# Rows loaded over 56 or 64 partitions instead of 53, and another order on VectorE, in a graph network's attention stage

## What is computed

```python
x = x * rsqrt(mean(x*x) + EPS) * rms_w          # 1250 x 1024
x = x @ W_down                                  # 1250 x 256
xl = (x @ Wl).reshape(n, 4, 64)                 # what a node sends
xr = (x @ Wr).reshape(n, 4, 64)                 # what a node adds as a receiver
# edges, and one loop for each node
msg = xl[src] + xr[dst]
act = where(msg > 0, msg, 0.2 * msg)
e = einsum('ehd,hd->eh', act, att)              # one score for each edge and head
m = segment_max(e, dst)
p = exp(e - m[dst])
out = segment_sum(p * xl[src], dst) / segment_sum(p, dst)
out = out.reshape(n, 256) @ W_up
```

## Time and profile before

| | |
|---|---|
| time before, median of 3 runs | 1694.56 us (1694.53 to 1698.33) |
| the profiled execution's own time | 1698.34 us |
| its span, first to last instruction | 1696.6 us |
| PE busy | 1495.4 us, 88% |
| DVE busy | 790.8 us, 47% |
| ACT busy | 442.5 us, 26% |
| POOL busy | 245.4 us, 14% |
| mean granted TensorE clock | 0.961 |

### The profile page before, as it was taken

The page is one execution under the profiler, slowest core; times in us unless marked ns, Lnnn a source line. Parts: engine busy times, 40 slices in busy tenths (PEclk is TensorE's granted clock), DMA queues, the critical chain, the costliest instruction groups (busy, mean ns, idle before and its releaser), DMA issues.

```text
span 1696.6 us, 19105 instructions
## 1 busy us (share of the span) xinstructions
PE 1495.4 (88%) x7184; PEld 1193.5 (70%) x7184; DVE 790.8 (47%) x1352; ACT 442.5 (26%) x723; POOL 245.4 (14%) x298
## 2 busy tenths in 40 slices
PE   3898999506888888887999999999999999999996
PEld 2887888505555555555888888888888888888885
DVE  6996665201666766675444375223113332321233
ACT  7762222103445454542111111002011000210000
POOL 1000000005455544530000001001000010000000
PEclk9997999857999999999999999999999999999998
DMA  1655343013444435432321365224006654410153
GB/s 42 176 166 183 121 104 103 18 49 110 129 156 135 123 106 166 135 96 85 123 107 50 104 229 213 86 96 149 1 0 211 199 174 149 155 37 1 59 183 105
DMA packets 100425, 196.57 MB, mean 116 GB/s; under 512 B 25550, under 2 KB 59638, under 8 KB 100334
## 3 DMA queue, kind: packets, MB, share of 16 engines
q1 hardware_dynamic: 75720, 121.00, 23.2%
q0 software_dynamic: 22992, 74.13, 12.7%
q10 hardware_dynamic: 1622, 0.22, 0.1%
HBM read 141.39 MB, written 53.92 MB: 115 GB/s over the span
## 4 chain that ended last, share of the span: by engine, by line
PE 52%; DVE 0%; ACT 0%; issue 0%; POOL 0%; DVEq 0%
PE layers_y_ps L1764 33%; PE layers_y_ps L1785 16%; PE layers_turn_ps L1748 2%; PE layers_up_ps L1732 2%; PE layers_y_ps L1801 1%; PE layers_turn_ps L1720 0%; PE layers_y_ps L1809 0%; DVE layers_parts_lo L1932 0%; DVE layers_y L1965 0%; POOL out L1705 0%; ACT layers_parts_hi L1876 0%; DVE layers_y L625 0%; DVE layers_y L2027 0%; DVE layers_ln_stats L2031 0%; DVE layers_ln_stats L619 0%
## 5 line engine op out<-in xcount | busy, mean ns | idle before, releaser
L1785 PE MATMUL layers_y_ps<-layers_parts_hi,layers_counts 128*128 128x512 f32 x464 | 143.6, 391 | 0.0
L1170 POOL DMA_INDIRECT attention_got<-xl_d,attention_src x128 | 126.5, 989 | 116.6 <-DVE attention_weighted L1415 69.7
L1785 PE MATMUL layers_y_ps<-layers_parts_lo,layers_counts 128*128 128x512 f32 x464 | 143.3, 390 | 0.0
L1764 PE MATMUL layers_y_ps<-layers_w_hi,layers_parts_hi 128*128 128x512 f32 x400 | 125.9, 396 | 0.0
L1764 PE MATMUL layers_y_ps<-layers_w_lo,layers_parts_hi 128*128 128x512 f32 x400 | 123.6, 390 | 0.0
L1764 PE MATMUL layers_y_ps<-layers_w_hi,layers_parts_lo 128*128 128x512 f32 x400 | 123.5, 390 | 0.0
L1170 POOL DMA_INDIRECT attention_got<-xl_d,heads_first_src x64 | 63.7, 995 | 411.9 <-issue 371.2
L1236 PE MATMUL attention_mix_ps<-attention_weighted,attention_hot 128*106 128x260 f32 x384 | 101.6, 399 | 5.2 <-DVE attention_weighted L1415 5.1
L1236 PEld LDWEIGHTS attention_mix_ps<-attention_weighted,attention_hot 128*106 128x106 f32 x384 | 66.4, 178 | 52.7 <-DVE attention_weighted L1415 24.3
L1201 PE MATMUL attention_row_ps<-attention_bent,edges_att_rows 128*128 128x512 f32 x192 | 102.5, 617 | 0.0
L1363 DVE TENSOR_TENSOR attention_bent<-attention_message_ps,attention_scaled 128x512 f32<-128x512 f32 x96 | 65.8, 686 | 74.0 <-ACT attention_scaled L1300 54.0
(11 more groups left out here) (306 smaller groups left out, 2904.3 us busy)
## 6 DMA issues: line engine op xcount, KB each, us to landing
layers_counts<-counts_d SPq DMA_DIRECT2D x30, 640.0 KB, 4.0
heads_dst_wide<-in_dst_held SPq DMA_DIRECT2D x25, 512.0 KB, 5.9
layers_rest<-x_d SPq DMA_DIRECT2D x23, 512.0 KB, 4.1
x_d<-layers_y POOLq DMA_DIRECT2D x20, 512.0 KB, 2.9
self_d<-layers_y POOLq DMA_DIRECT2D x20, 512.0 KB, 5.5
fetched_x<-x_d SPq DMA_DIRECT2D x17, 512.0 KB, 3.6
fetched_raw<-in_L_gnn_W_self POOLq DMA_DIRECT2D x16, 512.0 KB, 5.7
fetched_raw<-in_L_gnn_W_neigh POOLq DMA_DIRECT2D x16, 512.0 KB, 8.6
```

The source lines that it names most:

```text
L1170: pool.indirect_dma_start(got[s][:, t, :], None, xl_d, bass.IndirectOffsetOnAxis(src[s][:, t:t + 1], 0))\
L1764: last = nc.tensor.matmul(y_ps[n % 2][:, a:a + HALF], rows_in[t][:, k * P:(k + 1) * P], w[k][:, a:a + HALF], start=(k == 0 and p == 0), st ...
L1785: last = nc.tensor.matmul(y_ps[n % 2][:, a:a + HALF], counts[c % 2][:, k, :], part[k][:, a:a + HALF], start=(k == 0 and part is hi), stop= ...
```

## The change

Five edits. (1) `own_messages` reads and writes 56 partitions instead of 53 (`OWN_ROWS`). (2) `own_scores` takes 64 (`PART`) instead of 53, except for group 21, whose 39 rows stay; `last_scores` takes 25, 64 and 48 rows. (3) attention's xr rows are loaded over 64 partitions (32 for the last group). The rows beyond 53 belong to the next group; what they bring reaches no output. `summed` gets 64 partitions. (4) VectorE's order within a visit: both `weigh` go ahead of `bend` in unit 0, `take_max` 0 and 1 ahead of it in unit 2, `take_max` 3 and `take_best` ahead of it in unit 3, and `finish(j - 3)` moves from unit 1 to the end of unit 3. (5) ACT: `take_shifted` ahead of `keep_sums`.

```diff
+    LAST_ROW, OWN_ROWS = (BLOCKS - 1) * P, 56
...
         def own_messages(engine, first, end, heads):
-            span = slice(first * SUB, end * SUB)
-            own_xl = xl_d[span, :].rearrange("(j n) (h d) -> n j h d", n=SUB, h=HEADS)
             for h in heads:
-                engine.dma_start(summed[:, first:end, h, 0:HEAD_DIM], own_xl[:, :, h, :]).then_inc(g["own_loaded"], 16)
+                own_xl = bass.AP(xl_d.tensor, first * SUB * HID + h * HEAD_DIM,
+                                 [[HID, OWN_ROWS], [SUB * HID, end - first], [1, HEAD_DIM]])
+                engine.dma_start(summed[0:OWN_ROWS, first:end, h, 0:HEAD_DIM], own_xl).then_inc(g["own_loaded"], 16)
 
-        def own_scores(engine, first, end, nodes=SUB):
-            span = slice(first * SUB, first * SUB + (end - first) * nodes)
-            scores = loop_d[span, :].rearrange("(j n) (t k) -> t n j k", n=nodes, t=2)
+        def own_scores(engine, first, end, nodes=PART):
             for t in range(2):
-                engine.dma_start(best[t * PART:t * PART + nodes, first:end, :], scores[t])\
+                scores = bass.AP(loop_d.tensor, first * SUB * HEADS + t * KH,
+                                 [[HEADS, nodes], [SUB * HEADS, end - first], [1, KH]])
+                engine.dma_start(best[t * PART:t * PART + nodes, first:end, :], scores)\
                     .then_inc(g["own_loaded"], 16)
...
-                first, end = max(j * SUB, LAST_ROW), (j + 1) * SUB
+                first = max(j * SUB, LAST_ROW)
+                end = min(j * SUB + PART, first + 16 * ((ROWS - first) // 16))
...
+                held = min(PART, 32 * ((ROWS - j * SUB) // 32))
                 for part in range(2):
-                    sp.dma_start(xr[j % 3][part * PART:part * PART + SUB, :].bitcast(F32),
-                                 xr_d[part][j * SUB:(j + 1) * SUB, :]).then_inc(xr_ready[j % 3], 16)
+                    sp.dma_start(xr[j % 3][part * PART:part * PART + held, :].bitcast(F32),
+                                 xr_d[part][j * SUB:j * SUB + held, :]).then_inc(xr_ready[j % 3], 16)
...
                 if q == 3 and 1 <= j <= SUBS:
+                    take_shifted(j - 1)
                     keep_sums(j - 1)
-                    take_shifted(j - 1)
...
                 if q == 0 and 2 <= j <= SUBS + 1:
                     clamp(j - 2)
-                if i < LAST:
-                    bend(i)
-                if q == 0 and 2 <= j <= SUBS + 1:
                     weigh(j - 2, 0)
                     weigh(j - 2, 1)
-                if q == 1 and 3 <= j <= SUBS + 2:
-                    finish(j - 3)
                 if q == 2 and 1 <= j <= SUBS:
-                    for u in range(3):
-                        take_max(j - 1, u)
+                    take_max(j - 1, 0)
+                    take_max(j - 1, 1)
                 if q == 3 and 1 <= j <= SUBS:
                     take_max(j - 1, 3)
                     take_best(j - 1)
+                if i < LAST:
+                    bend(i)
+                if q == 2 and 1 <= j <= SUBS:
+                    take_max(j - 1, 2)
+                if q == 3 and 1 <= j <= SUBS:
                     find_edges(j - 1)
                     keep_best(j - 1)
+                if q == 3 and 3 <= j <= SUBS + 2:
+                    finish(j - 3)
```

More of the change, by code:

```diff
@@ L632, in front_stage @@
     EARLY, CLEAR, LAST_FILL = BLOCKS - 3, 4, 48
-    LAST_ROW = (BLOCKS - 1) * P
+    LAST_ROW, OWN_ROWS = (BLOCKS - 1) * P, 56
     with ExitStack() as ctx:
@@ L1422, in finish @@
                 b = j % 2
-                whole = summed[:, j]
+                whole = summed[0:SUB, j]
                 dve.wait_ge(keep_ready, j + 1)
@@ L2141, in graph_layers @@
                 best = m.sb("best", [P, SUBS, KH])
-                summed = m.sb("summed", [SUB, SUBS, HEADS, HEAD_DIM + 1])
+                summed = m.sb("summed", [PART, SUBS, HEADS, HEAD_DIM + 1])
                 first_src = m.sb("first_src", [P, SUB_TILES], I32)
```

## The result

The changed kernel takes 1618.49 us (median of 4, 1617.55 to 1622.2) against 1696.32 for the kernel before beside it: 0.9545 of it, 95% interval 0.9524 to 0.9566, and the medians are 77.8 us apart. 87.6 less (1607) was forecast; the range (1580 to 1634) held the time.

What follows compares the result with a forecast made beforehand. TensorE, 88% busy overall, was taken as the bound, with stalls where SP's issues held its queue. A 42.4, B 13.5, C 12.4 and D 19.3 sum to 87.6 us less, from 1694.56 to 1607; range 1580 to 1634.

Steps and rivals of the forecast that it cites:

- Spreading: Front's end: with 56 and 64 rows the six SP issues take 0.5 us each, over at 298 us instead of 351.
- A: Front's end, to take_heads(9): ACT takes the product at 318.3 us instead of 360.76, 42.4 us less.
- B: From take_heads(9) to attention's start: 10 us instead of 23.5, so 13.5 us less.
- C: Attention's start to the first clamp: gathers 6.4 us less, TensorE's clock 6 us less, 12.4 us less in all.
- D: Attention's visits, first to last clamp: the new order makes 350.1 us into 330.8, 19.3 us less.
- the one on POOL: Visits: POOL's indices come 4.3 us late, but it has room, its 8 gathers taking 10.3 us of the visit.
- the forecast's own ring: Visits: finish, store, dst_wide's landing, find_nodes, bend and finish again set the pace, 9.15 + w, 13.75 us instead of 14.76.
- w: Visits: the landing time of dst_wide behind the store, taken as 4.6 us.
- TensorE's 12.3 us a visit: Visits: without its two waits for VectorE, 2.45 us a visit, TensorE could do a visit in 12.3 us instead of 14.76.
- R2: Visits: the order brings nothing, w being 5.6 us or more; time 1617 to 1638 us, chance 0.3.
- R3: Front's end: the transfers do not spread or pieces hold the issue; about 1692 us, no change, chance 0.03.
- R4: Visits: slower than before through SP's late load, needing 18.4 us in each of 19 visits; chance 0.02.

Runs made afterwards that it cites:

- e1: The changed kernel with both orders (VectorE's and ACT's) as before, keeping edits 1 to 3: 1628.48 us, 0.9578 of the kernel before.
- e3: The changed kernel with SP's store of a group put behind the next group's load instead of ahead of it: 1573.54 us, 0.9276 of the kernel before.
- e9: The changed kernel itself once more, on the chip of the last group of runs: 1620.36 us, 0.9559 of the kernel before.
- e2: The changed kernel with 53 rows everywhere, keeping only the two new orders (edits 4 and 5): 1685.5 us, 0.9944 of the kernel before.
- e5: The changed kernel with the next group's source indices (src) alone issued ahead of the store: 1610.82 us, 0.9463 of the kernel before.
- e6: The changed kernel with the next group's dst_wide alone issued ahead of the store: 1628.1 us, 0.9572 of the kernel before.
- e8: The changed kernel with attention's xr rows loaded over 53 partitions as before: 1629.43 us, 0.9593 of the kernel before.
- e12: e3 with the store issued in two pieces of 48 and 5 rows, as in e7: 1562.54 us, 0.9217 of the kernel before.
- e10: The changed kernel with ACT's keep_sums ahead of take_shifted again: 1624.15 us, 0.9577 of the kernel before.
- e7: The changed kernel with the store issued in two pieces of 48 and 5 rows: 1612.01 us, 0.9487 of the kernel before.

## Why the prediction was right, and where not

**Spreading: right.** The six issues take 6.4 us, 0.75 for a message and 1.7 for a score load, not 0.5 each. That was harmless: they end at 297.4, and the next store is not due until 302.5. A is 42.6 against 42.4, and e1 shows A, B and C (42.5, 15.5 and 8.9 us less) with neither order changed. With 53 rows the four message issues, of 848 pieces each, took 9.25 us each at a DMA share of 0.08 (295.24 to 332.20 us); with 56 rows, 896 pieces, they take 0.75, and the share over the front's end is 0.54. Neither the pieces nor the bytes had held them, then. Over how many engines a transfer goes no run here counts. That it is about one of the 16 with 53 rows is an estimate from the share alone, 0.08 against 1/16; that 56 and 64 rows spread is read from the issue times and the share. `summed` over 64 partitions costs an instruction nothing, as said: its memset takes 5.26 us over 53 (L1012) and over 64 (L1013).

**B and C: sizes.** B was 1.9 more (the short issues of both queues ended at 320.2). C was 2.0 less. Its two parts were 6.4 for the gathers and 6 for TensorE. Group 1's gathers now begin 10.7 us after the first (333.27) against 16.0 before, so 5.3 less; TensorE's work went from 31.0 to 25.5 us, 5.5 less, at a clock of 0.90. The first `bend` came 10.7 us after the first gather, as said.

**D: near in sum, by visits that the argument was not about.** 19 of the 23 visits (third clamp to the last but two) have a late load. The forecast had them at 19 x 13.75 + 18 = 279.3 us, and the other four at 51.5. Windows of the 19, before, after and in e3, with the columns of the earlier trace rows:

```profile
459.02:750.22 291.20, 238.95 (x1028) 154.40 (x1029) 202.86 (x480) 146.53 (x214) 151.50 (x152) 0.98 0.44 135
```

```profile
380.02:674.15 294.13, 245.52 (x1025) 160.36 (x1024) 201.99 (x481) 142.47 (x214) 149.18 (x153) 0.94 0.46 138
```

```profile
379.13:629.60 250.47, 230.32 (x1028) 149.95 (x1027) 199.86 (x482) 142.79 (x214) 153.10 (x153) 1.00 0.52 157
```

They gained nothing: 291.2 before, 294.1 after, 291.8 in e9. All of D's 9.3 us comes from the other four, 58.9 before and 46.7 after. e2 has it the same way, 289.9 and 47.9. That D came out with the right sign is thus luck as far as the ring goes.

The step that failed is the one on POOL: that its indices come 4.3 us late, "of which it has room: its 8 gathers take 10.3 of the visit". I set 10.3 us of gathers against one visit and left out that TensorE needs the last of them in unit 2, in the next visit, and that from the last gather's start to its landing it takes 5.6 us. What binds is another ring, that is, a chain of waits that comes back to the same piece of work. It closes over two visits (SP, POOL, PE and DVE of the changed kernel):

```profile
521.01 0.28 SPq L1131 DMA_DIRECT2D mixed_d<-attention_mixed  x1
522.37 0.36 SPq L1087 DMA_DIRECT2D attention_src<-in_src_held  x1
```

```profile
526.06 1.62 POOL L1172 DMA_INDIRECT attention_got<-xl_d,attention_src  x1 [4.58 <-DMA attention_src<-in_src_held]
...
535.53 1.69 POOL L1172 DMA_INDIRECT attention_got<-xl_d,attention_src  x1 [0.30 <-issue]
```

```profile
541.12 0.66 PE L1191 MATMUL attention_message_ps<-all_ident,attention_got 128*128 128x128 f32 x4 [2.92 <-DMA attention_got<-xl_d,attention_src]
```

```profile
549.20 0.42 DVE L1440 TENSOR_TENSOR attention_mixed<-heads_summed,attention_inverse 53x256 f32<-53x256 f32 x1
```

Finish to store to src 1.4 us, its landing 3.7, seven more gathers 9.5, the last one's work and landing 5.6, from unit 2's messages to the end of finish 8.5: 28.6 us for two visits, 14.3 each. Over the 19 visits the mean is 15.5. Two things are seen to lengthen them: a weight fetch behind the store (at 505.92 it puts the landing of src at 5.8 us instead of 3.7), and TensorE's clock. Both visits of the pair above ran at 1.00. In the visit before it (504.19 to 520.91) the clock was 0.90; TensorE had waited 3.82 us for a gather, and two score matmuls (L1203) behind that wait took 1.91 us instead of 1.02. Over the 19 visits the clock is 0.94 and TensorE busy 245.5 us, against 1.00 and 230.3 us in e3 for the same work. What each is worth no run separates.

Which ring binds is shown on one chip, in the 19 visits: e5, which cuts only the ring through src, took 278.3 us; e6, which cuts only the forecast's through dst_wide, 294.9; e8, which cuts neither, 294.2. e3 cuts both and gives back 43 us. How much of these 43 is the ring through src alone is not measured: the changed kernel did not run on e5's chip.

Of the forecast's own ring (9.15 + w) the term w was well sized: the page of the changed kernel has 4.7 us as the median from issue to landing of dst_wide, 4.6 was taken. Whether this ring binds once the other is cut is open. In e5 ACT waits for dst_wide in 8 visits, and a plain visit takes 14.1 us against 13.75, but on a chip where visits tied to no load took 14.0 too. That its 278.3 us lie so near the forecast's 279.3 therefore shows nothing.

**TensorE's 12.3 us a visit: right.** e12 has 12.45. The five visits with a weight split took 83.7 us before (16.6 to 17.1 each, a plain one 14.75) and 79.7 after. In the trace after they hide in the waits, as said; in e12, without these waits, such a visit is 1 us longer than a plain one. That the swap on ACT "is worth nothing" held in time within what is measured here (e10 against e9), but not by its reason: e10 shows a wait that `finish` in unit 3 makes and the swap avoids. That it would count once the gathers don't bind is not shown; the four visits without late loads speak for it.

**Rivals.** The time fell 1.5 us above my own band (1597 to 1617), into the one given to R2 (1617 to 1638). In the 19 visits it is R2's outcome, the order brings nothing, yet by another ring and not by w. R3 falls with the issues; R4 was never near: the longest visit took 17.9 us, not 18.4 each.

## What to carry to other kernels

Where an issue holds a queue for many us while the DMA share is low (here four for 37.0 us at 0.08), try the transfer with a few rows more than needed: here 56 instead of 53 made it 2.99 us. When a piece of work is moved to the end of a loop, list who waits for it in each queue and what stands behind that wait, and follow each such chain round to the same piece again, over as many visits as it takes; the longest ring is the new pace. Here the move cost 43 us through a store ahead of the next group's loads, and a few lines in SP's program gave it back. And check a forecast's parts against the stretch each is about: here a sum for the visits came near although the visits it argued about gained nothing.

## What the runs showed of the hardware

The chip of e5 to e8 ran the attention visits slower where nothing held them: 14.0 to 14.3 us between the first clamps of e7, which in the changed kernel and in e9 are 12.7 and 12.2 us apart under the same order. In e7 the turn's last matmul is recorded as ended 2.3 us before VectorE begins the clamp that waited for it; VectorE is idle for the last 1.82 us of them:

```profile
382.64 0.60 PE L1228 MATMUL attention_row_ps<-all_ident,attention_shifted_rows 128*128 128x128 f32 x4
...
385.51 0.19 DVE L1411 TENSOR_SCALAR attention_clamped<-attention_row_ps 128x32 f32<-128x32 f32 x1 [1.82 <-remote]
```

Such waits, which end by "remote", stand 14 to 17 times ahead of the clamp in each of e5 to e8, and never in the traces of the other runs. The kernel before lost only 0.3% there (1700.57 against 1694.83 us). The cause is open; it is why e7's gain is given by its ratio alone, and e12 stands beside it.
